# x transposed in 32-row blocks on VectorE and exchanged through DRAM, where TensorE transposed it

## What is computed

```python
x = x + tanh(g_xattn[0]) * xattn(layernorm(x), ctx, mask, position_bias, ln_weight, w_q, w_k, w_v, w_out)
x = x + tanh(g_ffn[0]) * ffn(layernorm(x), base_W, base_b, router_W, router_b, A, B, expert_map)

def xattn(hidden, kv, ...):
    x   = rmsnorm(hidden, ln_weight)
    h_q = x @ w_q.T                       # 1024 tokens x 4096
    h_k = kv @ w_k.T
    h_v = kv @ w_v.T
    ...
```

## Time and profile before

| | us |
|---|---|
| runs | 839.34, 839.46, 838.26 |
| median | 839.34 |
| time of the profiled execution | 837.85 |
| its span, first to last instruction | 836.1 |
| PE busy in the span | 822.1 (98%) |
| DVE, ACT, POOL busy | 490.2, 426.1, 349.7 |

### The profile page before, as it was taken

How to read it: one execution, slowest core, us unless ns; L and a number is a source line. 1 busy time by engine, 2 the same in 40 slices (tenths; PEclk the granted TensorE clock), 3 DMA queues, 4 the chain that set the end, 5 groups by cost and what they waited for, 6 DMA issues and landing times.

```text
span 836.1 us, 13267 instructions
## 1 busy us (share of the span) xinstructions
PE 822.1 (98%) x4204; PEld 700.1 (84%) x4204; DVE 490.2 (59%) x918; ACT 426.1 (51%) x1057; POOL 349.7 (42%) x224
## 2 busy tenths in 40 slices
PE   6999999999999999999999999999999999999988
PEld 5888888888888888888888888888888888888866
DVE  6666656763443325656555666556555666668854
ACT  6567676676676655544444444444444444444110
POOL 0354544654465552434434444344434444342322
PEclk9999999999999999999999999999999999999999
DMA  8655555668555575776666666666566666744002
GB/s 305 198 170 152 163 153 152 174 184 264 171 156 173 166 216 152 229 209 207 187 198 199 195 208 186 180 191 176 178 197 188 190 184 184 223 142 148 14 26 76
DMA packets 147198, 147.60 MB, mean 177 GB/s; under 512 B 10960, under 2 KB 109392, under 8 KB 146768
## 3 DMA queue, kind: packets, MB, share of 16 engines
q1 hardware_dynamic: 147152, 147.02, 58.0%
HBM read 94.55 MB, written 52.43 MB: 176 GB/s over the span
## 4 chain that ended last, share of the span: by engine, by line
PE 96%; DVE 3%; issue 0%; DMA 0%; ACT 0%; SPq 0%; DVEq 0%
PE Sb L1496 7%; PE Ab L1507 7%; PE Sb L1348 7%; PE Sb L1350 7%; PE Sb L1349 7%; PE Vb L1339 4%; PE Vb L1340 4%; PE Vb L1341 4%; PE Ob L1339 4%; PE Ob L1341 4%; PE Ob L1340 4%; PE Kb L1339 4%; PE Kb L1340 4%; PE Kb L1341 4%; PE Ab L1348 3%; PE Ab L1350 3%
## 5 line engine op out<-in xcount | busy, mean ns | idle before, releaser
L528 POOL TENSOR_TENSOR bm<-bias,maskneg 128x512 f32<-128x512 f32 x64 | 83.6, 1307 | 174.7 <-DVE s_sb L1064 174.7
L750 ACT ACTIVATE p_exp<-s_sb,negmax 128x128 f32<-128x128 f32 x256 | 99.8, 391 | 76.9 <-DVE negmax L1066 76.9
L491 POOL TENSOR_TENSOR w_lo<-w_raw,w_hi 128x1280 fp32r<-128x1280 f32 (+1 forms) x29 | 86.9, 2995 | 118.3 <-ACT w_hi L620 118.3
L620 ACT ACTIVATE A_hi<-Ab 128x512 fp32r<-128x512 f32 x64 | 38.2, 597 | 163.5 <-PE Ab L1507 163.5
L1064 DVE TENSOR_TENSOR s_sb<-Sb,bm 128x512 f32<-128x512 f32 x62 | 42.8, 691 | 122.9 <-PE Sb L1496 122.9
L620 ACT ACTIVATE U<-Sb 128x512 f32<-128x512 f32 x90 | 53.9, 599 | 66.0 <-PE Sb L1350 65.5
L519 POOL TENSOR_TENSOR o_lo<-o_raw,o_hi 128x512 fp32r<-128x512 f32 x32 | 52.4, 1638 | 45.0 <-ACT o_hi L620 45.0
L1507 PEld LDWEIGHTS Ab<-pT,V 128*128 128x128 f32 x512 | 66.9, 191 | 5.0
L620 ACT ACTIVATE w_hi<-w_raw 128x512 fp32r<-128x512 f32 (+2 forms) x67 | 60.0, 899 | 21.2 <-PE Kb L1350 8.5
L1348 PE MATMUL Sb<-t_hi,w_lo 128*128 128x512 f32 x180 | 70.1, 389 | 0.0
L1350 PE MATMUL Sb<-t_hi,w_hi 128*128 128x512 f32 x180 | 70.0, 389 | 0.0
(11 more groups left out here) (278 smaller groups left out, 2119.5 us busy)
## 6 DMA issues: line engine op xcount, KB each, us to landing
qk_units<-unit_out SPq DMA_DIRECT2D x128, 256.0 KB, 2.9
qk<-qk_units SPq DMA_DIRECT2D x64, 512.0 KB, 4.6
p_rows<-p_blocks SPq DMA_DIRECT2D x64, 256.0 KB, 2.4
pT<-p_rows SPq DMA_DIRECT2D x256, 64.0 KB, 3.0
w_raw<-wqk SPq DMA_DIRECT2D x31, 512.0 KB, 4.1
v_raw<-wv SPq DMA_DIRECT2D x32, 256.0 KB, 4.0
o_raw<-wo SPq DMA_DIRECT2D x32, 256.0 KB, 3.8
stage<-ctxT SPq DMA_DIRECT2D x8, 256.0 KB, 5.2
```

Source lines behind the costliest of these rows:

```text
L491: pool.tensor_tensor(w_lo[:, n % 2, first:5, :], w_raw[:, n % 2, first:5, :], f32(w_hi[:, n % 2, first:5, :]), ALU.subtract).then_inc(w1_l ...
L528: pool.tensor_tensor(bm[:, :, :], bias4[:, q, :, :], maskneg[:, b:b + 1, :].broadcast_to([P, HU, S]), ALU.add).then_inc(bm_done, 1)
L620: act.activation(dst, src, ACT.Copy).then_inc(done, 1)
L750: last = act.activation(p_exp[:, i, :], s_sb[:, i, :], ACT.Exp, bias=negmax[:, i:i + 1], accum_out=rowsum[:, i:i + 1])
```

## The change

`x_transpose` moves from PE to DVE: after `normed(j)` DVE transposes the tile by 32x32 blocks into `x_blocks` (SBUF, two buffers). SP stores that to the DRAM tensor `x_rows` (`store_x`) and loads it back as `xT` in SBUF (`load_x`, four DMAs). ACT's `x_evict` and DVE's `x_tile_lo` read `xT` in place of the PSUM bank. Each tile is split two jobs after it was normed (before: one). Tiles 5 and 6 are both normed in job 10, and tile 7 in job 11 (before: jobs 10, 11 and 12), so that the last split stays in job 13; `centred` of tiles 5 and 6 is in job 9, of tile 7 in job 10. The identity is waited for later, at its first remaining use.

```diff
-        xT_bank = QP[:, :]
+            x_blocks, xT = sb_a("x_blocks", [P, 2, Q32, DC, 32]), sb_a("xT", [P, 2, Q32, DC, 32])
+        def x_exchanged(j, kept):
+            chunks = xT[:, j % 2, :, :, :].rearrange("p i c r -> p c i r")
+            return chunks[:, 2:4, :, :] if kept and j >= BH else chunks
+        NORMED = {5: (0,), 6: (1,), 7: (2,), 8: (3,), 9: (4,), 10: (5, 6), 11: (7,)}
...
+            def store_x(j):                                              # SP
+                reached(sp, ld_xT[j % 2], 16 * Q32 * (j // 2))
+                sp.wait_ge(xb_done, j + 1)
+                sp.dma_start(x_rows[j % 2, :, :, :].rearrange("p j n -> p (j n)"),
+                             x_blocks[:, j % 2, :, :, :].rearrange("p j c r -> p (j c r)")).then_inc(x_stored, 16)
+            def load_x(j):
+                sp.wait_ge(x_stored, 16 * (j + 1))
+                reached(sp, x_lo_done, j - 1)
+                for k in range(Q32):
+                    sp.dma_start(xT[32 * k:32 * k + 32, j % 2, :, :, :].rearrange("q i c r -> q i (c r)"),
+                                 x_rows[j % 2, :, k, :].rearrange("(i q) n -> q i n", i=Q32)).then_inc(ld_xT[j % 2], 16)
             for n in range(JOBS + 1):
                 if 0 < n and n + 2 < JOBS:
                     load_w(n + 2)
+                if NORMED.get(n - 1):
+                    load_x(NORMED[n - 1][-1])
...
                 if n < JOBS:
                     store(R11, n)
+                for j in NORMED.get(n, ()):
+                    store_x(j)
+                    if j != NORMED[n][-1]:
+                        load_x(j)
...
             def x_evict(j):                                              # ACT
-                act.wait_ge(xt_psum, j + 1)
+                act.wait_ge(ld_xT[j % 2], 16 * Q32 * (j // 2 + 1))
-                act.activation(c_columns(stage, j), xT_bank.rearrange("p (c n) -> p c n", c=DC),
-                               ACT.Copy).then_inc(xev_done, 1)
-                high(x_columns(x_hi, j), x_columns_psum(j), x_hi_done)
+                act.activation(by_block(c_columns(stage, j)), x_exchanged(j, False), ACT.Copy).then_inc(xev_done, 1)
+                high(by_block(x_columns(x_hi, j)), x_exchanged(j, True), x_hi_done)
...
-                if 6 <= n < 6 + B:
-                    x_evict(n - 6)
+                for j in NORMED.get(n - 2, ()):
+                    x_evict(j)
-                if 4 <= n < 4 + B:
-                    centred(n - 4)
+                for j in {9: (5, 6), 10: (7,)}.get(n, (n - 4,) if 4 <= n < 9 else ()):
+                    centred(j)
...
+            def x_transpose(j):                                          # DVE
+                dve.wait_ge(xn_done, j + 1)
+                reached(dve, x_stored, 16 * (j - 1))
+                dve.transpose(x_blocks[:, j % 2, :, :, :].rearrange("p j c r -> p c j r"),
+                              xn_at[j % BH].rearrange("p (c j q) -> p c j q", c=DC, j=Q32)).then_inc(xb_done, 1)
             def x_tile_lo(j):
                 dve.wait_ge(x_hi_done, j + 1)
-                low(x_columns(x_lo, j), x_columns_psum(j), x_columns(x_hi, j), x_lo_done)
+                low(by_block(x_columns(x_lo, j)), x_exchanged(j, True), by_block(x_columns(x_hi, j)), x_lo_done)
...
-                if 6 <= n < 6 + B:
-                    x_tile_lo(n - 6)
+                for j in NORMED.get(n - 2, ()):
+                    x_tile_lo(j)
-                if 5 <= n < 5 + B:
-                    normed(n - 5)
+                for j in NORMED.get(n, ()):
+                    normed(j)
+                    x_transpose(j)
...
-            def x_transpose(j):                                          # PE
...
-                for c in range(DC):
-                    last = pe.transpose(xT_bank[:, c * P:(c + 1) * P], xn_at[j % BH][:, c * P:(c + 1) * P],
-                                        ident[:, :])
-                last.then_inc(xt_psum, 1)
...
                 m5(n)
                 m7(n)
-                if 5 <= n < 5 + B:
-                    x_transpose(n - 5)
```

More of the change, by code:

```diff
@@ L52, in build @@
 def build(nc, x, ctxT, mask, g_xattn, g_ffn, bias, lnw, wqk, wv, wo, baseT, base_b, loraR, router_b,
-          lora_B, expert_map, qk_units, p_rows, out):
+          lora_B, expert_map, qk_units, p_rows, x_rows, out):
     with ExitStack() as ctx:
@@ L192, in build @@
         mean_done, scale_done, centred_done = sem("mean_done"), sem("scale_done"), sem("centred_done")
-        hidden_done, xn_done, xt_psum, xev_done = (sem(n) for n in ("hidden_done", "xn_done", "xt_psum", "xev_done"))
+        hidden_done, xn_done, xb_done, xev_done = (sem(n) for n in ("hidden_done", "xn_done", "xb_done", "xev_done"))
+        x_stored, ld_xT = sem("x_stored"), [sem("ld_xT0"), sem("ld_xT1")]
         x_hi_done, x_lo_done = sem("x_hi_done"), sem("x_lo_done")
@@ L258, in x_columns, with by_block @@
             return t[:, 0:2, :, b].rearrange("p k c n -> p (k c) n") if j < BH else t[:, 2, :, b]
-        def x_columns_psum(j):
-            chunks = xT_bank.rearrange("p (c n) -> p c n", c=DC)
-            return chunks if j < BH else chunks[:, 2:4, :]
+        def by_block(columns):
+            return columns.rearrange("p c (i r) -> p c i r", i=Q32)
+        def x_exchanged(j, kept):
+            chunks = xT[:, j % 2, :, :, :].rearrange("p i c r -> p c i r")
+            return chunks[:, 2:4, :, :] if kept and j >= BH else chunks
+        NORMED = {5: (0,), 6: (1,), 7: (2,), 8: (3,), 9: (4,), 10: (5, 6), 11: (7,)}
         def c_tile(t, j, c):
@@ L1011, in normed @@
                 dve.wait_ge(centred_done, j + 1)
-                reached(dve, xt_psum, j - 3)
+                reached(dve, xb_done, j - 3)
                 dve.scalar_tensor_tensor(out=xn_at[j % BH], in0=acc[:, j, :], scalar=norm_scale[:, h, i:i + 1],
                                          in1=row_bc[:, :], op0=ALU.mult, op1=ALU.mult).then_inc(xn_done, 1)
+            def x_transpose(j):
[3 more added lines that the diff above has]
+                              xn_at[j % BH].rearrange("p (c j q) -> p c j q", c=DC, j=Q32)).then_inc(xb_done, 1)
             def x_tile_lo(j):
                 dve.wait_ge(x_hi_done, j + 1)
-                low(x_columns(x_lo, j), x_columns_psum(j), x_columns(x_hi, j), x_lo_done)
+                low(by_block(x_columns(x_lo, j)), x_exchanged(j, True), by_block(x_columns(x_hi, j)), x_lo_done)
             def x_sum(k, a, b, before):
@@ L1432, in m7 @@
                 blocks(X[n % 2], n, S3, t_hi[:, T3, :, :], t_lo[:, T3, :, :], False, m_done[7])
-            def x_transpose(j):
[L1435 to L1440, removed]
-                for c in range(DC):
-                    last = pe.transpose(xT_bank[:, c * P:(c + 1) * P], xn_at[j % BH][:, c * P:(c + 1) * P],
-                                        ident[:, :])
-                last.then_inc(xt_psum, 1)
             def v_half(u, g, b, q, k):
@@ L1492, in scores @@
                     pe.wait_ge(s_done, 1 if isinstance(u, int) and u == 1 else u - 1)
+                if isinstance(u, int) and u == 0:
+                    pe.wait_ge(unit_done[R22], 1)
                 if isinstance(u, int) and EARLY <= u < 2 * EARLY:
@@ L1513, in y_transpose @@
                 if j == 0:
+                    pe.wait_ge(ident_done, 1)
                     pe.wait_ge(f_x1, 2)
@@ L1719 @@
     args.append(nc.dram_tensor("p_rows", (2, P, Q32, HU * 32), F32, kind="Internal").ap())
+    args.append(nc.dram_tensor("x_rows", (2, P, Q32, DC * 32), F32, kind="Internal").ap())
     args.append(nc.dram_tensor("out", (P, B, D), F32, kind="ExternalOutput").ap())
```

## The result

The changed kernel takes 842.33 us (median of 11 runs, 839.87 to 843.87) where the kernel before takes 839.2 (11 runs beside it, 837.79 to 839.92): a ratio of 1.0038, 95% interval 1.0028 to 1.0047. It is 3.1 us slower; 2.4 were forecast.

What follows compares the result with a forecast made beforehand. PE, busy 98% of the span, was taken to bound the kernel. Removed transpositions -3.92, waits in jobs 8 to 11 +3.8, jobs 13 to 16 +2.5 gave +2.4 on 839.34: 841.7 us, range 835.8 to 844.6 (8 in 10).

Steps and rivals of the forecast that it cites:

- The gain: On PE's path: eight transpositions removed at 0.49 us each, 3.92 us off, jobs going from 10.01 to 9.52 us.
- `x_lo` held by POOL: On DVE: with both inputs in SBUF `x_lo` waits out POOL's subtraction, adding 0.61 us a job, 0.34 for small tiles.
- The circle: Hand-overs over ACT, POOL and DVE from U3 to next U3: 8.50 + 0.90 + 0.61 = 10.01 us against PE's 9.52.
- the slack: At `m4`: U3 may be late by 1.92 us, once, before PE waits; job 7 uses it up.
- job 11, a small tile: 0.22: Job 11's hand-overs over DVE, ACT and POOL, with one small tile, exceed PE's 9.52 us by only 0.22.
- the queue's rival: On SP: late `store_x` holds back a `unit_out` store, ACT waits; 0.5 us in seven jobs, 845.2 us; chance 0.1.
- jobs 13 to 16, 2.5 us taken from 0 to 5: Last jobs, with sums of x tiles: lateness carried on costs PE 0 to 5.0 us, the middle, 2.5, taken.
- x_lo not held: Rival on DVE: `x_lo` runs free beside POOL, 9.40 us stays hidden, time 835.4 to 836.4 us; chance 0.24.
- Even: Rival: PE waits as forecast, but jobs 13 to 16 absorb the lateness; -0.1 us, 839.2 us; chance 0.2.
- SP's queue: Rival on SP: `store_x` delays a `unit_out` store that ACT needs; 3.5 us over seven jobs, 845.2 us; chance 0.1.

Runs made afterwards that it cites:

- e9: Changed kernel with `x_lo` moved from DVE to POOL and `load_x` behind SP's stores of R22 and R11: 835.39 us, ratio 0.9955.
- e1: Changed kernel with `x_lo` reading its first input from PSUM instead of SBUF (values left wrong): 836.73 us, ratio 0.9973.
- e4: Changed kernel with the `x_lo` subtraction moved from DVE to POOL, ahead of its last low parts of the weights: 836.15 us, ratio 0.9961.
- e7: Changed kernel with every block transpose on DVE done twice: 846.04 us, ratio 1.0086.
- e2: Changed kernel without the DRAM round trip, ACT and DVE reading the block transposes directly (x not fully transposed): 840.68 us, ratio 1.0018.
- e8: Changed kernel with `load_x` behind SP's stores of R22 and R11 instead of ahead of them: 841.19 us, ratio 1.0027.
- e3: Changed kernel with DVE's `c12` done ahead of `x_lo` and the other work on x: 837.69 us, ratio 0.9988.
- e11: Changed kernel with tiles 4 and 5 normed in job 9, 6 in job 10, 7 in job 11: 841.85 us, ratio 1.0027.
- e10: Changed kernel with `c12` ahead of the work on x, and `store_x` and `load_x` behind all four `unit_out` stores: 835.61 us, ratio 0.9965.

## Why the prediction was right, and where not

**The gain** is as worked out: jobs 5 to 7 last 9.52 us, and in e9, where nothing else is lost, 3.87 of 3.92 us come off.

**`x_lo` held by POOL** is right, and it decides (e1 and e4). It was to last 1.5 to 2.5 us and end 0.49 behind POOL, or 0.22 when small; a single one lasted 2.46 to 2.52 in the changed kernel's held jobs and ended 0.54 to 0.56 behind, or 0.28 when small. `t_lo` was the right row to go by. The Trainium skill (SBUF — State Buffer, Who interferes with whom) says that a DVE instruction with two SBUF inputs contends with a GpSimd one that reads SBUF, and that one with at most one such input, outside the two-port modes, does not. These runs agree, 2.52 us against e1's 0.69.

**The circle.** Forecast from U3 to U3 from job 8 on: 10.46, 10.08, 11.57, 9.74. Measured: 10.35, 10.07, 11.58, 10.65. The first three are right within 0.11 us, and with them jobs 9, 10 and 11 (0.82, 0.55 and 1.91 us lost for 0.94, 0.56 and 2.05). Part of that is luck: a transpose cost the circle 0.75 us, not 0.90 (e7), and in job 10 the 0.30 that two of them saved were made up by the second `xn`, held 0.29 us by POOL's last part. That job 7 would use up the slack came out as well, but by two sizes that were both off: U3 stood 1.71 us into job 8, not 2.12, and the slack was smaller than 1.92. `m4` starts 0.13 us after U3's end (96.87 to 97.00 in job 9), and of the 0.82 us lost in job 9 only 97.00 - 93.75 - 2.72 = 0.53 stand ahead of `m4`; the rest are later starts of the matmuls behind.

**The step that failed first: "job 11, a small tile: 0.22".** PE lost 1.90 us in job 12. Of this 10.65 - 9.52 = 1.13 came at `m4` and behind it, since POOL's last part held `xn` too (1.77 us for 0.74); I had POOL's first part alone in the circle, and didn't ask where the last part falls once everything is late. The other 0.77 came at `m7`: two tiles normed in one job are two `x_evict` pairs ahead of U2 two jobs later (ACT's timeline has them from 132.25 to 134.00, and U2 at 134.86, 6.29 behind U3 where one pair makes it 5.46 in job 11), which I had counted as costing nothing. Jobs 9 to 12 so lost 5.2 us, not 3.8.

**The step that failed second: jobs 13 to 16, 2.5 us taken from 0 to 5.** They lost 0.77. I let the lateness be carried into job 13. But the circle of job 12 took 8.64 us while PE's job took 11.42, and U3 was back at 0.20 of job 13 (137.21 - 137.01). What was lost there had the cause of the queue's rival, one 1.00 us wait of ACT behind `load_x`, and a sum on DVE held by POOL's last part; without the exchange (e2) or with `load_x` later (e8) it is nothing.

**The sum.** 3.92 off and 5.95 on, for 6.3 forecast: the two misses were opposite and nearly cancelled. So the forecast of 841.7 stands near 842.33 partly by luck, while its direction and mechanism were argued.

**The rivals.** *x_lo not held* is out in this kernel, and e1 shows what it would have been: 836.73, near the 835.4 to 836.4 given. *Even* was right in its part: jobs 13 to 16 do absorb the lateness, but for 0.77 us. *SP's queue* was there, but for 0.8 us and in one job, not for 3.5 in seven; it counts for more once the circle is cured (1.64 us in e3).

**Open.** The median of the changed kernel is 3.1 us over that of before, the profiled stretches differ by 2.10, and the two profiled executions by 839.87 - 837.85 = 2.02. The other microsecond lies in executions that were not profiled. A wait there that lowers PE's clock, as in e7 and e11, is not enough to explain it: of the eleven executions four have the mean granted clock of the profiled one, 0.998 (e7 and e11, with the clock lowered for some us, have 0.994), and they took 839.87, 841.57, 842.33 and 843.38 us. Why the stores of e10 took twice their usual time to land is open too, and was not tried further.

## What to carry to other kernels

When work is moved off the engine that bounds a kernel, write down the circle of the engines that take it, from one hand-over to the next, and compare it with the time that the bound engine will have afterwards, not with the time it had. Look at where each operand lies: one subtraction whose input moved from PSUM to SBUF decided here between 2.5 us gained and 3.1 lost, and the cure was to put it on the engine that it had been waiting for. Once a slack is used up, check again which instructions now fall beside each other, since in the late jobs other pairs met than in the early ones.
